# Attention operands stacked from SBUF to SBUF by twelve transfers per pair, instead of through DRAM

## The reference

```python
y = conv1d(mean(x, (2, 3)), w_c)                      # over channels
yc = sigmoid(x * y)
sa = sigmoid(conv2d(concat(mean_c(yc), max_c(yc)), w_s))
x = yc * sa + x
xn = groupnorm(x, 32 groups) * gn_w + gn_b
q, k, v = split(qkv_w @ xn + qkv_b)                   # 4 heads of 16
attn = softmax(q^T k / 4)                             # 256 x 256 per head
out = x + proj_w @ (attn @ v) + proj_b
```

## Time and profile before

| | |
|---|---|
| time, median of 3 runs | 187.82 us (187.49 to 189.54) |
| time of the profiled execution | 188.28 us |
| its span, first to last instruction | 186.5 us |
| PE busy | 167.9 us (90%) |
| DVE, ACT, POOL busy | 141.5, 120.4, 112.3 us |
| chain that ended last | PE 67%, DMA 10%, DVE 6%, POOL 6% |

### The profile page before, as it was taken

One profiled execution on the slowest core, in us unless ns is written; L12 is line 12 of the kernel. 1 busy time (PEld: TensorE's weight loads), 2 busy tenths in 40 slices (PEclk: granted clock), 3 DMA queues, 4 the chain that ended last, 5 costly groups with the idle time before them and its releaser, 6 DMA issues.

```text
span 186.5 us, 4811 instructions
## 1 busy us (share of the span) xinstructions
PE 167.9 (90%) x1518; PEld 105.6 (57%) x1518; DVE 141.5 (76%) x295; ACT 120.4 (65%) x250; POOL 112.3 (60%) x214
## 2 busy tenths in 40 slices
PE   7788985998786999999999999999999999998791
PEld 2255765464463577675766767676675655553230
DVE  0838669378866298998989899898997979777433
ACT  3072641452376387978988798898877967648730
POOL 5992184679685537888788788878876270101110
PEclk9969999999999699999999999999999999999967
DMA  3941403668279655556364564646554563310001
GB/s 76 357 136 40 114 7 101 184 202 221 86 226 223 184 116 162 156 184 172 119 199 129 193 177 156 191 124 192 159 174 133 178 207 102 99 33 29 23 11 56
DMA packets 20070, 26.25 MB, mean 141 GB/s; under 512 B 4268, under 2 KB 16980, under 8 KB 20052
## 3 DMA queue, kind: packets, MB, share of 16 engines
q1 hardware_dynamic: 19472, 25.47, 47.0%
q10 hardware_dynamic: 580, 0.55, 1.1%
HBM read 17.35 MB, written 8.42 MB: 138 GB/s over the span
## 4 chain that ended last, share of the span: by engine, by line
PE 67%; DMA 10%; DVE 6%; POOL 6%; issue 4%; ACT 3%; SPq 2%; POOLq 0%; ACTq 0%
PE bank L710 16%; PE bank L684 14%; PE bank L696 13%; PE bank L720 7%; PE bank L739 5%; DMA qs<-maxrow 4%; PE bank L730 3%; PE bank L623 2%; DMA parts_dram<-parts 2%; DMA con<-consts 2%; DMA ks<-parts_dram 2%; DVE maps L477 1%; PE bank L752 1%; POOL tapprod L308 1%; ACT pt L424 1%
## 5 line engine op out<-in xcount | busy, mean ns | idle before, releaser
L560 DVE TENSOR_REDUCE negmax<-bank 128x2 bf16<-128x512 f32 x128 | 83.5, 679 | 18.9 <-PE bank L684 17.4
L424 ACT ACTIVATE pt<-bank 128x512 f32<-128x512 f32 x128 | 72.8, 595 | 24.7 <-PE bank L696 24.7
L696 PE MATMUL bank<-qs,ks 97*128 97x256 bf16 x256 | 49.4, 275 | 5.3 <-DMA qs<-maxrow 3.3
L684 PE MATMUL bank<-ks,qs 96*128 96x256 bf16 x256 | 49.8, 276 | 1.9 <-DMA ks<-parts_dram 1.2
L710 PE MATMUL bank<-pt,vs 128*32 128x256 f32 x512 | 35.7, 399 | 0.0
L684 PEld LDWEIGHTS bank<-ks,qs 96*128 96x128 bf16 x256 | 21.7, 100 | 24.3 <-DVE negmax L560 15.5
L696 PEld LDWEIGHTS bank<-qs,ks 97*128 97x128 bf16 x256 | 23.7, 98 | 13.5 <-ACT pt L424 5.6
L321 POOL TENSOR_TENSOR xall<-yo,xall 128x256 f32 (+1 forms) x15 | 10.9, 725 | 31.2 <-ACT yo L444 31.2
L348 POOL TENSOR_TENSOR rest<-z,parts 128x512 f32<-128x512 f32 x15 | 17.3, 1155 | 11.1 <-issue 8.1
L710 PEld LDWEIGHTS bank<-pt,vs 128*32 128x32 f32 x512 | 15.2, 112 | 12.8 <-ACT pt L424 3.1
L600 PE MATMUL bank<-warm 128*128 128x512 bf16 x60 | 20.1, 452 | 1.4 <-POOL warm L298 1.4
(11 more groups left out here) (70 smaller groups left out, 215.6 us busy)
## 6 DMA issues: line engine op xcount, KB each, us to landing
parts_dram<-parts SPq DMA_DIRECT2D x48, 128.0 KB, 2.1
ks<-parts_dram SPq DMA_DIRECT2D x16, 192.0 KB, 3.0
qs<-parts_dram SPq DMA_DIRECT2D x16, 192.0 KB, 3.2
xall<-x SPq DMA_DIRECT2D x4, 512.0 KB, 5.9
qs<-parts_dram SPq DMA_DIRECT2D x16, 128.0 KB, 2.7
ks<-parts_dram SPq DMA_DIRECT2D x16, 128.0 KB, 2.7
out<-xall SPq DMA_DIRECT2D x16, 128.0 KB, 2.1
gate<-gate_dram SPq DMA_DIRECT2D x6, 256.0 KB, 3.9
```

The costliest lines, as they stand in the source:

```text
L424: nc.scalar.activation(pt[:, (u + LEAD) % UNITS, :, :].rearrange("p t n -> p (t n)"), st_bank[u % 2][:, :], ACT.Exp, scale=SCALE).then_inc ...
L560: nc.vector.tensor_reduce(negmax[:, slot(1), column:column + TILES], s_bank[u % 2][:, :].rearrange("p (t n) -> p t n", t=TILES), AX.X, ALU ...
L684: mm = pe.matmul(s_bank[u % 2][:, t * N:(t + 1) * N], qs[0:KQ, slot(1), h, a, t * P:(t + 1) * P], ks[0:KQ, slot(1), h, a, :], start=True, ...
L696: mm = pe.matmul(st_bank[u % 2][:, t * N:(t + 1) * N], ks[0:KQ + 1, slot(d), h, a, t * P:(t + 1) * P], qs[0:KQ + 1, slot(d), h, a, :], sta ...
```

## The change

The DRAM tensor and its writes and reads go. Instead `stack(d, part)` moves each part straight from `parts` to each slot that holds it. Part 0 has three slots in `qs` and three in `ks`, part 1 two and two, part 2 one and one. Each transfer reads 64 partitions of 1 KB and writes 16 partitions with four runs of 1 KB, 64 KB in all; there are twelve per pair.

The turn of SP is now: the maximum row of pair `k`; four transfers of part 1 and two of part 2 of pair `k+2`; the store of pair `k-3`; in turns 0 and 1 two gate reads; six transfers of part 0 of pair `k+3`, issued once part 1 of that pair is there (before turn 1: once part 0 is). On POOL the wait for `st_ready` moves ahead of three small operations of the normalisation (L354 to L358). One wait on ACT goes, and PE counts twelve transfers in place of six.

```diff
+TERMS = ((0, 0), (1, 0), (2, 0), (0, 1), (1, 1), (0, 2))
-        parts_dram = nc.dram_tensor("parts_dram", [RING, 3, 2, HD, HEADS * 2 * N], BF16).ap()
-            aside = {(0, 2): lambda: gate_read(sp, 2), (1, 2): lambda: gate_read(sp, 3)}
+            aside = {(0, 1): lambda: gate_read(sp, 2), (1, 1): lambda: gate_read(sp, 3)}
             def turn(k, slot, has, lap):
...
+                def stack(d, part):
+
+                    r = slot(d)
+                    for row, terms in enumerate(TERMS):
+                        for tile, g in ((qs, 0), (ks, 1)):
+                            if terms[g] == part:
+                                sp.dma_start(tile[row * HD:(row + 1) * HD, r, :, :, :].rearrange("p h a n -> p h (a n)"),
+                                             parts[C * g:C * (g + 1), r, part, :]).then_inc(stack_in[r], 16)
+
-                if has(2):
-                    wait(sp, parts_out[0], 16 * (k + 3))
-                    stack(ks, 1, 0, 3, part=0)
-                    stack(qs, 0, 5, 1)
                 if has(0):
                     wait(sp, mrow_ready, k + 1)
...
                 if has(2):
-                    wait(sp, parts_out[1], 16 * (k + 3))
-                    stack(qs, 0, 3, 2)
-                    stack(ks, 1, 3, 2, part=1)
-                    wait(sp, parts_out[2], 16 * (k + 3))
-                    stack(qs, 0, 0, 3)
-                    stack(ks, 1, 5, 1, part=2)
-                if has(3):
-                    wait(sp, p1_ready, k + 4)
-                    part_write(0)
+                    wait(sp, split_step, 3 * (k + 2) + 2)
+                    stack(2, 1)
+                    wait(sp, split_step, 3 * (k + 3))
+                    stack(2, 2)
                 if has(-3):
                     wait(sp, out_ready, k - 2)
...
+                stands_in(aside, k, 1)
                 if has(3):
-                    wait(sp, split_step, 3 * (k + 3) + 2)
-                    part_write(1)
-                    wait(sp, split_step, 3 * (k + 4))
-                    part_write(2)
-                stands_in(aside, k, 2)
+                    if isinstance(k, int) and k < 1:
+                        sp.wait_ge(p1_ready, k + 4)
+                    else:
+                        wait(sp, split_step, 3 * (k + 3) + 2)
+                    stack(3, 0)
...
@@ POOL
+                if on_pool:
+                    wait(pool, st_ready, UNITS * k)
                 if has(4):
                     wait(pool, rstd_ready, k + 5)
...
-                    wait(pool, st_ready, UNITS * k)
                     wait(pool, split_step, 3 * (k + 3) + 2)
@@ ACT
-                        wait(act, parts_out[0], 16 * k)
@@ PE
-                        wait(pe, stack_in[slot(1)], lap(1) * 96)
+                        wait(pe, stack_in[slot(1)], lap(1) * 2 * SLOTS * 16)
```

More of the change, by code:

```diff
@@ L157, in program @@
         split_step = sem("split_step")
-        parts_out, stack_in = [sem(f"parts_out{i}") for i in range(3)], [sem(f"stack_in{r}") for r in range(RING)]
+        stack_in = [sem(f"stack_in{r}") for r in range(RING)]
         s_ready, max_done = sem("s_ready"), sem("max_done")
```

## The result

| | before | after |
|---|---|---|
| median | 188.68 us | 204.82 us |
| profiled execution | 188.28 us | 203.47 us |
| its span | 186.5 us | 201.7 us |

The medians are of four executions each. The executions of a kernel on one chip fall into a quicker and a slower group (here 187.49 to 189.54 against 192.12 before, 202.63 and 203.47 against 206.17 and 208.94 after), and every ratio in this text compares the quicker group alone. The changed kernel is slower: the ratio is 1.078, with a 95% interval of 1.063 to 1.094. I had forecast 196.0 and a range of 187 to 203; the median lies above it. So the direction was right, and the size was half of what came: 8.1 us forecast in the profiled execution, 15.2 measured (203.47 - 188.28).

A forecast was written before the change was run, and what follows sets the result against it. PE bounded the kernel before; SP's issue queue would bound it after. Stack issues 93.6, other per-turn costs 16.6 and long issues 5.75 us after 46.9 gave 162.85, moving the end by 8.1 us: forecast 196.0 us, range 187 to 203.

The forecast's parts named there:

- That SP's queue becomes the bound: Steady turns: SP's issues take 8.4 us a turn, over PE's 7.95, so SP sets the pace; chance 0.73.
- d: Price of one new SBUF to SBUF issue on SP, taken as 0.56 us, or 0.60 with the gap.
- My ranking by shape: Earlier rows ranked by likeness in reshaping; nearest were the maximum row (0.53 us) and the filter bands (0.595).
- M(13): Start of the maximum row's issue in turn 13, forecast at 162.85 us.
- M(0): Start of the maximum row's issue in turn 0, forecast at 46.9 us.
- the long issues: Seven SP issues, 5.75 us over their like in all, assumed to be where SP's next instructions load; kept at seven.
- The fill: First turns: removing the DRAM trip gives back at most four PE waits and the slow clock, 5.5 us.
- Late landing: Rival: SP keeps up but the stack lands late, binding from a 3.25 us landing; about 189 us; chance 0.04.
- T(14): Start of turn 14's first score matmuls on PE, forecast at 169.3 us, against 161.16 before.
- Cheap issue: Rival: an issue costs under 0.5 us, SP keeps its slack, the gain is 5.1 us: 182.7; chance 0.14.
- Keeping pace: Rival: at 0.49 to 0.53 us per issue, steady loss and fill gain offset: 186 to 190 us; chance 0.09.
- my own dearest case: Upper bound of the SP-bound case: d = 0.60 with 0.2 us more waits per turn, shift 17, 205 us.

The follow-up runs named there:

- the first probe: Program computing nothing, SP issuing six transfers of each of ten forms: 128 plain rows 0.601 us per issue, fold 0.594, half size fold 0.594, store to DRAM 0.447.
- the second: Program computing nothing, SBUF and DRAM sides varied, in bursts and alone: DRAM loads 0.432 and 0.420 us in a burst, against 0.601 for plain rows from SBUF.
- two of the edits: Kernel before with the maximum row issued by ACT, in all turns or only in turns 0 to 2: 186.5 us, ratio 0.999, and 185.98 us, ratio 1.001.

## Why the prediction was right in sign and short in size

**That SP's queue becomes the bound: right.** The queue is full in the trace of the steady turns, and the runs with two issues less, with the row elsewhere, with half the bytes, and with four issues more on the old kernel each went the way that only this theory has.

**The price d: the term that was mis-sized.** This is the step of the forecast that failed most. I took d = 0.56 as the middle of 0.53 and 0.595; it was 0.593. The 0.53 of the maximum row was that of an issue with free time before it. In the changed kernel, in a row of issues, the same issue costs 0.591. My ranking by shape was wrong by the first probe, and both its neighbours were rows with both sides in SBUF, which is what counts by the second. With 156 transfers, 0.033 us each are 5.1 us.

**The sum, term by term.** M(13), the row of turn 13, was forecast at 162.85 and came at 171.55, 8.7 us later. M(0) gave 1.26 of it, turns 0 to 2 gave 1.4, turns 3 to 12 gave 6.7 (9.06 a turn without the long issues, against 8.39), and the long issues took 0.66 back (5.09 against 5.75). Of the 8.7 the price d is the largest part, with 5.1. In a clean turn of 8.97 the 0.58 over my 8.39 are 0.42 for the stack, 0.05 for the row and 0.11 for waits and gaps that I had estimated at 0.15.

**The fill: wrong.** I let turn 0 start 0.60 sooner, at 45.93. It started at 47.41, later than before, behind a wait of 0.93 for the stack:

```profile
47.41 0.38 PE L671 MATMUL bank<-ks,qs 96*128 96x256 bf16 x2 [0.93 <-DMA ks<-parts]
```

The transfer that it waited for, the last of pair 1, was issued at 42.31 and took 4.96 us to land, where I had assumed 3.0 at most. These are its line in the chain that ended last, the busy share of the DMA engines in 40 slices, and the gate reads on ACT's queue:

```profile
42.31 4.96 DMA ks<-parts
...
DMA  4940413394373532323232323323232323210001
...
gate<-gate_dram ACTq DMA_DIRECT2D x2, 256.0 KB, 5.1
```

In the ninth slice, 40.3 to 45.4 us, the DMA engines are full. The seven stack transfers issued from 39.1 to 43.0 took 4.4 to 5.4 us to land, where the median of the steady turns is 2.6, and the two gate reads, issued at 38.7 and 39.4, were in flight with them. So in the fill it was the landing that set the time, the mechanism of my rival *Late landing*, more than SP's issue time. The kernels above that have the same fill show the same (landings of 4.6 to 5.0 by the median there), but no run moves the gate reads away from it, so their share is not shown. SP was late too: it was free at 47.18 and not at 45.1, since its first issue came 0.5 later, 30 issues cost 0.035 more each, and one was 0.45 longer. That alone would have moved M(0) by 0.3.

**From the row to the next turn: right in length.** I had 6.4 us from M(13) to T(14). It was 6.32, though PE's last wait in it is for the stack, which I had said would not bind. It binds in nearly every turn, by 0.3 to 0.9 us, beside the wait for the row; this costs nothing more, since SP issues both:

```profile
177.87 0.38 PE L671 MATMUL bank<-ks,qs 96*128 96x256 bf16 x2 [0.80 <-DMA ks<-parts]
```

T(14) was 16.7 us later than in the earlier trace rows, and the end 15.2: the last 25.3 us of before, with a stretch at half clock, became 23.8 without one.

**The rivals.** *Cheap issue* had 0.14 and rested on the part writes' 0.34. The probes show why that row could not speak for the new transfers: it has a side in DRAM, and it is an issue with some free time around it. The probes' bursts with one side in DRAM show 0.42 to 0.45, and those from SBUF to SBUF 0.59 to 0.60. The estimate of 0.43 us, from the Trainium skill, "DMA: Bandwidth & Descriptors" (the table of fast descriptor generation) with the clock of "Advanced Engine Details and Errata", Clock Domains, agrees with the first and not with the second. *Keeping pace* needed d under 0.53. *Late landing* is refuted for the steady turns by the half bytes, but it is what happened to the first turn.

**The range.** Its upper end lay at 203, below my own dearest case of 205, to leave out two cases in ten. The forecast's own bounds, 191 to 205, held the result; the range that I gave didn't. Both ends of d were rows of before, and a count of 156 turns the 0.035 us from the middle to the upper one into 5.5 us.

## What to carry to other kernels

Count the transfers that a queue issues in one turn and multiply by the price of an issue in a row, not by that of one with free time around it; when the product passes the turn of the busiest engine, the queue is the bound, and here half the bytes changed nothing. Here 11 issues of 6 us fitted in 7.95 and 14 of 8.97 didn't, and two less, or two moved to another engine's queue, brought the steady turn back to 7.95. A way through DRAM that needs fewer issues can beat a direct one that needs more.

## What the runs showed of the hardware

- An issue on SP costs 0.59 to 0.60 us in a burst when both sides are in SBUF, for 16 to 128 rows and 16 to 128 KB, and 0.42 to 0.45 when one side is in DRAM and both are plain rows. Alone it is 0.47 (plain) or 0.55 (folded), and 0.31 to 0.33. The stack reads of before, from DRAM with more dimensions, cost 0.58 all the same.
- An issue of SP is 0.5 to 1.05 us longer where a 16 KB transfer stands on the queue that loads instructions: 14 of 15 long issues in the two traces, and none in the second lap of the loop.
- 128 rows folded into 16 partitions of eight runs took 5.1 us to land by the median of six in a burst, 64 rows into 16 partitions 2.6, and 128 plain rows 2.1. 64 rows on both sides took 2.0, and from 16 partitions into 64 it was 2.5. Few partitions on one side cost landing time; in the steady turns it didn't count.
- With the DMA engines full, from 40 to 46 us in the kernel after, such transfers took 4.4 to 5.4 us to land at 175 GB/s; the kernel before moved 240 GB/s in the same stretch at a share of 0.95.
- Equal runs of the kernel before lay between 183.4 and 190.9 us, as wide as most of the edits were worth. The profiled execution alone would have made two of the edits look 2 to 3% faster.
